# Diagonal gate matrices of a mixture-of-experts stage: from ScalarE, one in each step, to VectorE, four in one operation

## What is computed

```python
logits = x @ gate_w.T
probs = jax.nn.softmax(logits, axis=-1)
top2_p, top2_i = jax.lax.top_k(probs, 2)
w = top2_p / jnp.maximum(top2_p.sum(-1, keepdims=True), 1e-10)
...
moe_out = w[:, 0:1] * out0 + w[:, 1:2] * out1
result = jnp.clip(x + moe_out, -100.0, 100.0).reshape(Bb, Ss, Dd)
```

## Time and profile before

| | |
|---|---|
| median of 3 runs | 441.57 us (439.8 to 443.04) |
| span of the profiled execution | 510.3 us, 21148 instructions |
| mean granted TensorE clock over the span | 0.938 |
| PE busy | 420.0 us (82%) |
| DVE busy | 349.9 us (69%) |
| ACT busy | 327.5 us (64%) |
| POOL busy | 287.8 us (56%) |

### The profile page before, as it was taken

The page is one execution under the profiler, slowest core; times in us unless marked ns, Lnnn a source line. Parts: engine busy times, 40 slices in busy tenths (PEclk is TensorE's granted clock), DMA queues, the critical chain, the costliest instruction groups (busy, mean ns, idle before and its releaser), DMA issues.

```text
span 510.3 us, 21148 instructions
## 1 busy us (share of the span) xinstructions
PE 420.0 (82%) x8602; PEld 310.1 (61%) x8602; DVE 349.9 (69%) x910; ACT 327.5 (64%) x776; POOL 287.8 (56%) x483
## 2 busy tenths in 40 slices
PE   7696999998898899898898888496567787967991
PEld 2363566675585585585585455165557676866991
DVE  7984888997697697697698696256634454533286
ACT  5293887977777777777776657165446666655435
POOL 6032344557657657657657667524765665665542
PEclk9998999999999999999999999789668889888996
DMA  6644375565466466544444312501434333237134
GB/s 190 192 120 143 116 202 159 186 185 168 152 173 186 148 185 168 162 140 130 148 125 120 87 30 52 135 13 40 109 106 110 89 81 83 78 76 231 49 117 125
DMA packets 77664, 65.24 MB, mean 128 GB/s; under 512 B 12390, under 2 KB 72045, under 8 KB 77568
## 3 DMA queue, kind: packets, MB, share of 16 engines
q1 hardware_dynamic: 72624, 55.27, 38.4%
q0 software_dynamic: 4512, 8.54, 5.0%
q10 hardware_dynamic: 432, 0.07, 0.1%
HBM read 36.88 MB, written 25.46 MB: 122 GB/s over the span
## 4 chain that ended last, share of the span: by engine, by line
PE 57%; DVE 12%; issue 9%; ACT 6%; SPq 6%; another core or an unknown queue 5%; DMA 2%; POOL 2%; DVEq 0%; ACTq 0%; POOLq 0%
PE psum L1099 19%; PE psum L1191 11%; PE psum L1133 8%; PE psum L1354 6%; DVE nmax L1533 6%; PE psum L1369 5%; ACT probs L952 4%; PE psum L1440 3%; SPq L513 2%; PE psum L1146 2%; PE psum L1343 2%; PE psum L1432 1%; SPq L538 1%; DMA dq<-side 1%
## 5 line engine op out<-in xcount | busy, mean ns | idle before, releaser
L952 ACT ACTIVATE probs<-psum 128x512 f32<-128x512 f32 x320 | 182.5, 598 | 80.4 <-PE psum L1099 52.3
L1533 DVE TENSOR_REDUCE nmax<-psum 128x2 f32<-128x1024 f32 (+7 forms) x256 | 180.4, 746 | 50.5 <-remote 29.3
L1099 PE MATMUL psum<-qst,kst 128*32 128x128 bf16 (+3 forms) x2048 | 149.3, 303 | 22.6 <-issue 12.9
L836 POOL TENSOR_SCALAR_AFFINE_SELECT probs<-probs 128x512 f32<-128x512 f32 x180 | 81.8, 484 | 107.8 <-ACT probs L952 107.8
L1133 PE MATMUL psum<-kst,qst 128*32 128x288 bf16 (+15 forms) x2048 | 105.6, 281 | 7.1 <-DVE nmax L1533 4.0
L915 POOL DMA_INDIRECT o_dram<-probs,xs x77 | 77.6, 1007 | 58.4 <-DVE probs L1793 34.2
L1191 PE MATMUL psum<-probs,vst 128*32 128x256 f32 (+2 forms) x1280 | 105.6, 386 | 4.2 <-issue 3.5
L1099 PEld LDWEIGHTS psum<-qst,kst 128*32 128x32 bf16 x2048 | 61.0, 96 | 70.5 <-issue 35.3
L1146 PE MATMUL psum<-bmask,bident 128*32 128x64 bf16 (+2 forms) x1280 | 76.7, 198 | 0.8 <-issue 0.8
L1133 PEld LDWEIGHTS psum<-kst,qst 128*32 128x32 bf16 x2048 | 60.4, 96 | 21.2 <-issue 7.0
L1146 PEld LDWEIGHTS psum<-bmask,bident 128*32 128x32 bf16 x1280 | 45.1, 97 | 10.0 <-issue 2.8
(11 more groups left out here) (245 smaller groups left out, 690.8 us busy)
## 6 DMA issues: line engine op xcount, KB each, us to landing
kst<-dk SPq DMA_DIRECT2D x62, 128.0 KB, 3.5
qst<-dq SPq DMA_DIRECT2D x31, 256.0 KB, 4.4
xs<-xs_dram SPq DMA_DIRECT2D x77, 66.0 KB
dk<-side SPq DMA_DIRECT2D x7, 384.0 KB
dq<-side SPq DMA_DIRECT2D x7, 384.0 KB, 2.8
dk<-side SPq DMA_DIRECT2D x9, 256.0 KB, 3.0
side<-in_xT SPq DMA_DIRECT2D x8, 256.0 KB, 3.4
dq<-side SPq DMA_DIRECT2D x8, 256.0 KB, 2.7
```

Source lines behind the costliest of these rows:

```text
L836: pool.affine_select(out=view, in_=view, compare_op=ALU.is_ge, fill=0.0, base=0, pattern=[[0, view.shape[1]], [1, P]], channel_multiplier= ...
L952: act.activation(probs[:, c % 2, p, kk * T:(kk + 1) * T], psum[:, km_bank(b, c, k), :], ACT.Exp, scale=SCALE).then_inc(S["exp_done"], 1)
L1099: last = pe.matmul(out[32 * g:32 * g + 32], stationary[:, 32 * g:32 * g + 32], moving, skip_group_check=True, **flags)
L1533: last = dve.tensor_reduce(nmax[:, c, 2 * t:2 * t + 2], ps[:, :, at:at + TWO * (t + 1)], AX.X, ALU.max, negate=True)
```

## The change

The loop over tiles on ACT no longer makes diagonal matrices, and no longer waits for `gates` at step 14. DVE makes them instead, four at a time (the four groups of 128 tokens of one batch and one of the two experts) in one `tensor_tensor` over 512 columns: the identity matrix, read four times, multiplied by the gate weights, each spread over 128 columns. It does so at every third step, from step 16 to step 61, behind the weights of that step: 16 operations. `weighted(q)` counts 2 semaphore increments for each batch instead of 8.

```diff
-        DIAG_FROM = 14
+        DIAG_FROM, DIAG_STEP = 16, 3
...
-            def diagonal(n):
-                q, k, i = n // (TOPK * NQ), n // NQ % TOPK, n % NQ
-                act.activation(diag[:, q, k, i, :], ident[:], ACT.Copy,
-                               scale=gw[:, 4 + k, q * NQ + i:q * NQ + i + 1]).then_inc(S["diag_ready"], 1)
-
             for j in range(TAIL_DONE["copy"], NT + HLAG):
                 step(j, HLAG)
-                if j == DIAG_FROM:
-                    act.wait_ge(S["gate_link"], 8)
-                if DIAG_FROM <= j < DIAG_FROM + B * TOPK * NQ:
-                    diagonal(j - DIAG_FROM)
...
-                pe.wait_ge(S["diag_ready"], (q + 1) * TOPK * NQ)
+                pe.wait_ge(S["diag_ready"], (q + 1) * TOPK)
...
+            def diagonals(n):
+
+                q, k = n // TOPK, n % TOPK
+                if n == 0:
+                    dve.wait_ge(S["gate_link"], 8)
+                dve.tensor_tensor(diag[:, q, k, :, :], ident[:].unsqueeze(1).to_broadcast([P, NQ, P]),
+                                  gw[:, 4 + k, q * NQ:q * NQ + NQ].unsqueeze(2).to_broadcast([P, NQ, P]), ALU.mult
+                                  ).then_inc(S["diag_ready"], 1)
...
+                if j >= DIAG_FROM and (j - DIAG_FROM) % DIAG_STEP == 0 and (j - DIAG_FROM) // DIAG_STEP < B * TOPK:
+                    diagonals((j - DIAG_FROM) // DIAG_STEP)
```

## The result

The changed kernel takes 445.75 us (median of 20 runs, 442.83 to 451.74), the kernel before, beside it on the same chip, 442.17 us (median of 20, 439.38 to 446.97). The ratio is 1.0079, with a 95% interval of 1.0057 to 1.0100: slower, by 3.5 us, and within 1%, the case forecast. The predicted time was 442.5 us. Timed a second time, the ratio was 1.0080 (1.0042 to 1.0118). Ratios are taken over the fast runs of each kernel, those within about 1.5% of its fastest.

A forecast was written before the change was run, and what follows sets the result against it. No engine was full; unhindered, POOL was slowest at 1.27 us a step, while PE held 61.8% of the chain. Terms -1.7 + 0 + 2.2 + 0.45, about +1 us, on 441.57 gave 442.5 us, range 435 to 449.

The forecast's parts named there:

- the case forecast: Whole kernel: time stays within 1% (4.4 us) of the kernel before; chance 0.55.
- The order of paces: Tile loop, unhindered time per step: POOL 1.27 us, PE 1.00, ACT 0.95, DVE 0.83.
- the doubt about the stalls: Tile loop: unnamed stalls of 2 to 3.6 us in the profile may be fewer in a run without it.
- ACT, -1.7 us: Tile loop: PE's 6 waits for ACT each lose a 0.29 us matrix, gaining 1.7 us; bounds 0 and 6.9.
- DVE's pace, +2.2 us: Tile loop: 3.7 new operations of 0.6 us fall in DVE's backlog on the chain, costing 2.2 us; bounds 0 and 9.6.
- POOL's pace, +0.45 us: Tile loop: new DVE operations stretch POOL's scatters by 0.9 us, counted by half; bounds 0 and 10.6.
- The rival that named the mechanism: Tile loop: new DVE operations hold POOL's scatters, 2.6 us worked out, 10.6 at most; priced +6, 447.5 us; chance 0.07.
- DVE as the bound: Tile loop without stalls: DVE's 1.03 to 1.11 us a step sets the pace; priced +5.5, 447 us; chance 0.18.
- ACT in the way: Tile loop: ACT's delays reach PE, so relief removes 6.9 us of waits, giving 435 us; chance 0.20.
- What would show it: Profile signs: ACT copy to copy 0.66 us, new DVE operation 0.66 to 0.69, mean scatter little over 1.01 us.
- the port: DVE operations blocking POOL's scatters at SBUF; sign: mean scatter 1.1 us or more, long ones under new operations; chance 0.07.

The follow-up runs named there:

- before_again: The kernel before, unchanged, profiled a second time and without stalls: 440.09 us, profiled span 438.4 us.
- no_matrices: The kernel before with no matrices made on ACT or DVE; PE multiplies by the identity, leaving the gate weights out: ratio 0.9991 to the kernel before.
- act_kept: The changed kernel with ACT also making its 64 copies as before, into a buffer nothing reads: ratio 1.0042 to the kernel before.
- after: The first profile of the changed kernel, without stalls: span 441.1 us.
- one_input: No matrices, gate weights left out; at the changed kernel's 16 places DVE sums four readings of the identity, one SBUF input: ratio 0.9995 to the kernel before.
- short_matrices: The changed kernel with DVE making 64 matrices of 128 columns one at a time, gate weight as scalar per partition: ratio 0.9945 to the kernel before.
- two_input_twice: The changed kernel with each of the 16 matrix operations issued twice, the second result into a buffer nothing reads: ratio 1.0095 to the kernel before.

## Why the prediction was right, and where its sum was not

**What bounds the kernel.** The order of paces, with POOL's 1.27 us a step the slowest, before PE, ACT and DVE, was right, and so was the doubt about the stalls: without them the loop runs at POOL's pace (71.7 us for 54 sends in before_again, 1.33 a step, where the stalled profile had 1.67). The step that was missing is that the loads wait for sends, which makes POOL's pace the kernel's.

**ACT, -1.7 us: it was 0.** no_matrices (0.9991) and act_kept (1.0042, against 1.008) show no worth of ACT's time. The waits for ACT in the earlier trace rows are hardly there without the stalls: 0.2 us in before_again, 0.5 in after. ACT's idle time ahead of its copies and gelus grew instead, from 13.4 us in the stretch of the 54 sends in before_again to 25.3 in after.

**DVE's pace, +2.2 us: it was 0.** one_input costs nothing, and short_matrices has twice the work and is faster. The 11 steps of chain through DVE's backlog were read from behind the stalls as well; that the stalls made them is argued and not shown. These two terms were wrong together and nearly cancelled, by luck.

**POOL's pace, +0.45 us: it was 2.3 to 3.3.** This is the term that was mis-sized, by two choices. The first was to carry the loss of the copies over as an average, 0.08 us for each us of DVE's work. The changed kernel lost 0.20 and 0.30 us for each us added (2.2 and 3.3 by 10.9), since what counts is how much of one operation is left when a send starts, and that grows faster than the operation's length. The second was to count it by half. With POOL's 1.27 us standing first in my own list it counts in full.

**The rival that named the mechanism** had it right: the new operations hold POOL back. Its working, 16 x 0.5 x 0.33 = 2.6 us, is what the profiles show (2.2 to 3.3), and eight sends met one, as it had it (16 x 0.5). They lost 0.24 to 0.26 us each where it took 0.33; the rest, 0.3 and 1.2 us, lies at copies, which more sends met (16 and 17 in the two profiles of the changed kernel, 14 in before_again). The +6 us on which I then priced it, with a chance of 0.07, had no row behind it. The Trainium skill (SBUF — State Buffer, Who interferes with whom) says that a Vector instruction with two SBUF inputs contends with a GpSimd one that reads SBUF, that a copy can contend with GpSimd too, and that the order of issue decides which of the two blocks. The send of 1.55 us behind the operation of 0.67 and that of 2.10 behind 1.21 agree with the first; the send of 1.35 behind a copy and the copy stretched to 0.70 behind a running send agree with the others. Only as inferred, it adds that a `tensor_tensor` spares the descriptors of a DMA from POOL; the sends of 1.55 and 2.10 us were held, and the measurement decides. The section also says that on trn2 a reduce never contends, and one_input agrees: a send that began with 0.60 us of one left took 0.97.

**DVE as the bound** and **ACT in the way** both fall. POOL has no gap above 0.35 us even with the operations doubled, and the relief brought nothing.

**What would show it.** ACT never went from copy to copy in 0.66 us: 1.00 is the least in after as in before_again, the pace of PE's turns, so what ACT was freed of became idle time. The new operation takes 0.683 us with 0.60 to the next start, as foretold. The mean send was to stay little over 1.01 us if only the average counted, and 1.1 was to speak for the port. It came out at 1.065 and 1.084, nearer to the second, with the long sends under the new operations.

The forecast of no change beyond 1% held, since the loss is real but 0.8%. That is in part luck: of the three terms two measured nothing, and the one that counts was 5 to 7 times its 0.45 us; at 4.4 us it would have been out of the case.

What stays open: up to 1.2 us of the 3.5 lies outside the stretch that the profiles show, within what single runs differ by; the time of one_input against its profile; and which of length and kind of input makes the operations of short_matrices harmless where they were met.

## What to carry to other kernels

Find the engine whose work has no gap between its pieces and whose results somebody waits for; here it was POOL, at 66% of busy time less busy than PE, DVE and ACT. An operation put on DVE beside such a chain on POOL costs what is left of it when POOL's next DMA starts, so its length counts more than the sum of DVE's time: several short ones can cost less than one long one. If a profile has stalls that its time as run can't contain, take the paces and the order of waits from it, but no term of the sum that rests on a wait inside a stall.

## What the runs showed of the hardware

- An indirect DMA issued by POOL occupies it for 0.972 us, and the next one starts 0.30 us later, over 54 in a row (short_matrices). A copy from SBUF to SBUF on DVE, or a multiplication with both inputs in SBUF, that runs at its start adds nearly what is left of it: 0.38 us under a copy, 0.61 under a multiplication of 512 columns, 1.13 under one of 1024. Over all 13 profiles without stalls, POOL's indirect DMAs from 290 us on began 222 times at least 0.05 us behind the start of such an operation and with 0.2 us or more left of it; all but 3 lost 0.12 to 0.14 us less than was left, or 0.02 to 0.05 us less. Why there are two levels is open.
- A reduce with its input in SBUF adds nothing: a send that began with 0.60 us left of one took 0.97 us (one_input).
- An add with one input in PSUM, 0.29 us long, adds little: ten sends of before_again that began under one lost 0.1 us together.
- It works both ways: a copy that begins 0.59 us behind the start of a send lasts 0.70 us in place of 0.50 (short_matrices). One that begins 0.35 us behind it keeps its 0.50 (after, 369.61 us).
- Two engines can fall into step, so that the loss vanishes (0.0 us in short_matrices with 20 us of DVE work) or grows at operations that were there before (copies 2.6 us in before_again, 6.1 in two_input_twice).
- One profile of the kernel before had a span of 510.3 us with unnamed stalls, the next 438.4 without any.
